# Context attention: VectorE multiplies the probabilities by the reciprocal, GpSimd keeps the power and the bias

## The chip, the cores and the metric

The kernel runs on one core of one Trainium2 chip. The metric is the device time of one execution in microseconds (us). The engines are TensorE (PE, with its weight loads shown apart as PEld), VectorE (DVE), ScalarE (ACT), GpSimd (POOL) and SyncE (SP), which here only issues DMAs.

## What is computed

Two layers of gated cross attention and feed forward work on x, 8 batches of 512 rows with 512 columns, all float32. The change lies in the attention of the second layer, which attends over a context of 77 rows:

```python
x = x + tanh(g_xattn[0]) * L0_xattn(layernorm(x), fside, fside, ctx, ...)
x = x + tanh(g_ffn[0]) * L0_ffn(layernorm(x), ...)
x = x + tanh(g_xattn[1]) * L1_xattn(layernorm(x), ctx, ctx, ...)
x = x + tanh(g_ffn[1]) * L1_ffn(layernorm(x), ...)

# L1_xattn: 16 heads of 32
q, k, v = split_heads(Q @ Wq.T + bq), split_heads(K @ Wk.T + bk), split_heads(V @ Wv.T + bv)
attn = softmax(einsum('bhqd,bhkd->bhqk', q, k) / sqrt(d_k), axis=-1)
return einsum('bhqk,bhkd->bhqd', attn, v) merged over heads @ Wo.T + bo
```

The keys and values of the context come from an earlier pass.

## The kernel before

The program is a row of passes, one after another with a barrier between them: the context, the first attention, the quantised feed forward, the context attention (`context_attention_pass`, the pass of the change, names beginning with `xat_` in the profile), the recurrence and the output.

**Tiles.** A batch has T = 4 row blocks of P = 128 rows and C = 4 column blocks of 128. The 16 heads go in 4 groups c of HG = 4 heads. One group of one batch is a quad, numbered i = b * 4 + c. Its scores, 128 partitions x 4 heads x 4 row blocks x 77, are 1232 values a partition.

**One quad.** TensorE makes the scores in PSUM (L2081). VectorE takes the maximum, negated (L2221), and adds it to the scores, into SM in SBUF (L2224). ScalarE takes the exponential into E (L2165). VectorE sums E (L2231) and takes the reciprocal RD (L2233). GpSimd multiplies E by RD, broadcast over the 77, into PR (L2030). TensorE transposes PR head by head into PSUM (L2090), ScalarE copies each into PT (L2150), and TensorE multiplies the values with it (L2070, the job "att"). SM, E, SU, RD and PR have two buffers each, taken in turn by c % 2.

**The other jobs.** "x" are transposes of the normalised rows XN of the next batch (L2057), "q" the query projection (L108, from XT and WQ), "out" the output projection (L108, from AT and WO). Float32 operands of a projection are held as a high and a low half: ScalarE copies the high half out of PSUM (L2136 for x, L2145 for att), VectorE subtracts it for the low half (L2215). Queries are taken out by ScalarE with their bias (L2142). For "out" VectorE adds the gated product to the rows in XR (L2210); it waits for s_bo, the bias being in XR. The products of all jobs share two PSUM banks, so that a job waits until what stood two jobs before it has been taken out.

**The order.** It is written out by hand. A turn is one batch, with groups c = 0 to 3. TURN says which jobs stand in which group, with the lag of their batch, and SLOT between which of the 4 heads' transposes:

```python
TURN = [[("att", 2, -1), ("q", 3, 0), ("x", 0, 1), ("x", 1, 1), ("x", 2, 1), ("x", 3, 1)],
        [("att", 3, -1), ("q", 0, 1), ("out", 0, -1), ("out", 1, -1)],
        [("out", 2, -1), ("out", 3, -1), ("att", 0, 0)],
        [("att", 1, 0), ("q", 1, 1), ("q", 2, 1)]]
```

In group c TensorE transposes the quad before and, behind slot 1, makes the scores of the next one, for which VectorE must have read the present ones (s_sub). VectorE's queue in a group is: maximum and subtract, the jobs of slots 0 and 1, sums and reciprocal, the jobs of slots 2 and 3, and at the end of group 1 the statistics of the rows two batches ahead (L573 to L582), at the end of group 3 their scaling (L587, four instructions of 128x512 from X to XN). Between these two GpSimd computes the power -0.5 of the variance (L561). ScalarE's exponential stands at the start of slot 1.

**Rows in and out.** XR holds the rows to which the output is added. SyncE stores a batch when its four out jobs are taken (L1972, in group 2 of the turn after), then loads the next rows into XR (L1988). GpSimd adds the gated output bias BO to all of XR (L2035) in group 3, behind its multiply. In the last turn it then computes the power for the next pass, whose first rows VectorE scales at the end of group 3.

**The loop.** `clock` runs the same `group(b, c)` on every engine: turn 0 written out, turns 1 to 5 as a loop on the engine, turns 6 and 7 written out, with jobs ahead and late around them.

Of the kernel before, what the change touches and what calls it, by code (L numbers as in the profile page):

```python
# [9 lines left out]
ALU = mybir.AluOpType  # L10
# [3 lines left out]
P = 128  # L14
B = 8
S = 512
D = 512
T = S // P
# [3 lines left out]
HG = P // DH  # L22
G = 77
# [8 lines left out]
def f32(ap):  # L32
    return ap.bitcast(F32)
# [79 lines left out]
def make_identity(pool, ident, sem):  # L113
    pool.memset(ident, 0.0).then_inc(sem, 1)
    pool.wait_ge(sem, 1)
    pool.affine_select(out=ident, in_=ident, compare_op=ALU.not_equal, fill=1.0, base=0,
                       pattern=[[-1, P]], channel_multiplier=1).then_inc(sem, 1)
# [1711 lines left out]
def context_attention_pass(nc, x2_s, g, bq, bo, k1_s, v1_s, x3_s, next_w, WQ, WO, X, XN, NEXT):  # L1829
# [23 lines left out]
    def jobs_of(turn, c):  # L1853

        here = MIDDLE if not isinstance(turn, int) else turn
        return [(kind, i, turn + lag) for slot in range(T) for kind, i, lag in TURN[c]
                if SLOT[kind, i] == slot and 0 <= here + lag < B]
# [22 lines left out]
    with Pass(nc, "xat") as ps:  # L1880
# [3 lines left out]
        BO = ps.sb("bo", [P, D])  # L1884
        TG = ps.sb("tg", [P, 2])
        XR = ps.sb("xr", [P, T, D])
# [7 lines left out]
        E = [ps.sb(f"e{i}", [P, HG * T, G]) for i in range(2)]  # L1894
        SU = [ps.sb(f"su{i}", [P, HG * T]) for i in range(2)]
        RD = [ps.sb(f"rd{i}", [P, HG * T]) for i in range(2)]
        PR = [ps.sb(f"pr{i}", [P, HG, T, G]) for i in range(2)]
# [7 lines left out]
        s_x, s_xr, s_v, s_store, s_dve = (ps.sem(n) for n in ("x", "xr", "v", "store", "dve"))  # L1905
# [3 lines left out]
        s_xhi, s_ahi, s_bo = (ps.sem(n) for n in ("xhi", "ahi", "bo_added"))  # L1909
        s_s, s_neg, s_sub, s_exp, s_sum, s_rd, s_nrm = (  # L1910
            ps.sem(n) for n in ("s", "neg", "sub", "exp", "sum", "rd", "nrm"))
        s_pt, s_pte = ps.sem("pt"), ps.sem("pte")
# [5 lines left out]
        def wait_some(eng, sem, value):  # L1918

            if not isinstance(value, int) or value > 0:  # L1920
                eng.wait_ge(sem, value)

        def bank(turn, job):
            return pj_ps[place(turn, job)[0] % 2][:]

        def clock(eng, group, ahead, late):

            ahead()
            for c in range(C):
                group(0, c)  # L1930
            with eng.Fori(0, B - 3) as i:
                for c in range(C):
                    group(i + 1, c)
            for b in (B - 2, B - 1):
                for c in range(C):
                    group(b, c)
            late()

        def quad(b, c):
            return b * C + c  # L1940
# [72 lines left out]
        @block.gpsimd  # L2013
        def _(pool):
            make_identity(pool, ident[:], s_ident)
            ln.pool_setup(pool)
            pool.sem_inc(ln.s_rstd, 1)

            def ahead():
                ln.pool_power(pool, 1)  # L2020
                pool.wait_ge(s_act0, 1)
                pool.tensor_scalar(BO[:], BO[:], TG[:, 1:2], None, ALU.mult).then_inc(s_pool, 1)
                pool.wait_ge(s_pool, 1)

            def group(b, c):
                last = isinstance(b, int) and b >= B - 2
                i = quad(b, c)
                pool.wait_ge(s_rd, i + 1)
                wait_some(pool, s_pt, i * HG - HG)
                pool.tensor_tensor(PR[c % 2][:].rearrange("p j t g -> p (j t) g"), E[c % 2][:],  # L2030
                                   RD[c % 2][:].unsqueeze(2).broadcast_to([P, HG * T, G]),
                                   ALU.mult).then_inc(s_nrm, 1)
                if c == 3:
                    pool.wait_ge(s_xr, b * 16 + 16)
                    pool.tensor_tensor(XR[:], XR[:], BO[:].unsqueeze(1).broadcast_to([P, T, D]),  # L2035
                                       ALU.add).then_inc(s_bo, 1)
                if c == 2 and not last:
                    ln.pool_power(pool, b + 2)
                if c == 3 and isinstance(b, int) and b == B - 1:
                    ln.pool_power(pool, B)  # L2040

            clock(pool, group, ahead, lambda: None)
# [155 lines left out]
        @block.vector  # L2198
        def _(dve):
            dve.sem_inc(s_dve, ln.DVE_N)  # L2200
            dve.sem_inc(ln.s_var, 1)

            def job(turn, task):

                kind, i, b = task
                src = bank(turn, task)
                if kind == "out":
                    dve.wait_ge(s_bo, b + 1)
                    dve.wait_ge(made["out"], b * C + i + 1)
                    dve.scalar_tensor_tensor(XR[:, i, :], src, TG[:, 1:2], XR[:, i, :],  # L2210
                                             ALU.mult, ALU.add).then_inc(taken["out"], 1)
                elif kind != "q":
                    halves, high = {"x": (XT, s_xhi), "att": (AT, s_ahi)}[kind]
                    dve.wait_ge(high, b * C + i + 1)
                    dve.tensor_tensor(halves[1][:, i, :], src, f32(halves[0][:, i, :]),  # L2215
                                      ALU.subtract).then_inc(taken[kind], 1)

            def minus_max(b, c):
                i = quad(b, c)
                dve.wait_ge(s_s, i + 1)  # L2220
                dve.tensor_reduce(MX[c % 2][:], s_v4, AX, ALU.max, negate=True).then_inc(s_neg, 1)  # L2221
                dve.wait_ge(s_neg, i + 1)
                wait_some(dve, s_exp, i - 1)
                dve.tensor_tensor(SM[c % 2][:], s_v4, MX[c % 2][:].unsqueeze(3).broadcast_to([P, HG, T, G]),  # L2224
                                  ALU.add).then_inc(s_sub, 1)

            def sums(b, c):
                i = quad(b, c)
                dve.wait_ge(s_exp, i + 1)
                wait_some(dve, s_nrm, i - 1)  # L2230
                dve.tensor_reduce(SU[c % 2][:], E[c % 2][:], AX, ALU.add).then_inc(s_sum, 1)  # L2231
                dve.wait_ge(s_sum, i + 1)
                dve.reciprocal(RD[c % 2][:], SU[c % 2][:]).then_inc(s_rd, 1)  # L2233

            def normalise(b, part, first=False):

                me = Steps(s_dve, b, ln.DVE_N)
                if part == 0:
                    dve.wait_ge(s_x, b * 16 + 16)
                    ln.moments(dve, me)  # L2240
                else:
                    me.done = 2 * T + 1
                    dve.wait_ge(made["x"], b * C)
                    ln.scale(dve, b, me)

            def next_low(n):

                dve.wait_ge(s_nexthi, n + 1)
                dve.tensor_tensor(NEXT[n][1][:], STAGE[:], f32(NEXT[n][0][:]), ALU.subtract).then_inc(s_nextlo, 1)

            def group(b, c):
                last = isinstance(b, int) and b >= B - 2
                jobs = jobs_of(b, c)
                minus_max(b, c)
                for j in range(HG):
                    if j == 2:
                        sums(b, c)
                    for task in jobs:
                        if SLOT[task[:2]] == j:
                            job(b, task)  # L2260
                    if not last and j == 3 and c in (1, 3):
                        normalise(b + 2, c // 2)
                at = (b - B + 2) * C + c if isinstance(b, int) else -1
                if 0 <= at < 6 and at % 2:
                    next_low(at // 2)
                if isinstance(b, int) and b == B - 1:
                    if c == 2:
                        dve.wait_ge(s_nextx, 16)
                        ln.moments(dve, Steps(s_next, 0, ln.DVE_N))
                    if c == 3:  # L2270
                        after = Steps(s_next, 0, ln.DVE_N)
                        after.done = 2 * T + 1
                        dve.wait_ge(made["x"], B * C)
                        ln.scale(dve, B, after)

            def ahead():
                for task in AHEAD:
                    job(-1, task)
                for part in range(2):
                    normalise(1, part)  # L2280
                dve.wait_ge(s_act0, 1)

            def late():
                for task in LATE:
                    job(B, task)

            clock(dve, group, ahead, late)
# [509 lines left out]
```

## Time and profile before

| | us |
|---|---|
| median of 3 runs (2578.31 to 2589.29) | 2588.45 |
| the profiled execution, its own time | 2587.03 |
| its span, first to last instruction | 2585.2 |
| busy: PE, DVE, ACT, POOL | 2362.0, 1443.2, 1060.5, 608.7 |
| mean granted clock of TensorE | 0.962 |

Columns of the groups below: start in us from the span's start, duration, engine and line, operation, the tiles it writes and reads, their sizes in partitions x elements, how many instructions a row merges, and in brackets how long the engine sat idle before it and what ended that. A granted clock of 1.00 is TensorE's level of 2.4 GHz, 0.50 that of 1.2 GHz.

### The profile page before, as it was taken

What the parts mean: (1) busy time and instruction counts of PE and PEld (TensorE: products, weight loads), DVE (VectorE), ACT (ScalarE), POOL (GpSimd) and SP (SyncE); (2) the same over time, 40 slices, a digit from 0 to 9 for tenths busy, and PEclk for the clock granted to TensorE, in tenths of its full rate; (3) what the DMA queues carried; (4) which work ended last, traced back from release to release, by engine and by line L of the source; (5) the groups of instructions that cost most, each with busy time, mean ns of one, the idle gap of its engine ahead of it and who ended that gap; (6) DMA issues with size and microseconds to landing.
All of it is one profiled execution on the core that took longest, in us unless ns stands there. A gap on an engine that the chain in (4) does not pass through costs nothing. (4 is left out here: it accounts for less than half of the span.)

```text
span 2585.2 us, 40732 instructions
## 1 busy us (share of the span) xinstructions
PE 2362.0 (91%) x16307; PEld 1554.4 (60%) x16348; DVE 1443.2 (56%) x1747; ACT 1060.5 (41%) x1228; POOL 608.7 (24%) x208
## 2 busy tenths in 40 slices
PE   8899999999999987899999878898878999999989
PEld 6655554555555543444444346676656888888867
DVE  7665646556565545777777567878544222222235
ACT  5444445444454442555554534444423221121223
POOL 0045546455464651000000013323210000000000
PEclk9899999999999988999999989999879999999999
DMA  9410101101010103111111131212322000000046
GB/s 298 178 40 12 49 10 48 43 11 47 10 48 11 56 15 123 34 50 49 49 53 38 38 112 44 83 56 87 106 85 82 33 32 26 22 32 32 17 156 218
DMA packets 102015, 163.73 MB, mean 63 GB/s; under 512 B 16997, under 2 KB 39525, under 8 KB 99103
## 3 DMA queue, kind: packets, MB, share of 16 engines
q1 hardware_dynamic: 95918, 150.82, 17.6%
q10 hardware_dynamic: 6000, 11.54, 1.2%
q8 instruction: 71, 1.16, 0.2%
q14 instruction: 26, 0.21, 0.0%
HBM read 112.63 MB, written 49.71 MB: 63 GB/s over the span
## 5 line engine op out<-in xcount | busy, mean ns | idle before, releaser
L1135 DVE TENSOR_REDUCE att_mx<-att_sn 128x2 f32<-128x1024 f32 x256 | 313.6, 1225 | 168.4 <-PE att_sn L947 166.0
L1047 ACT ACTIVATE att_num<-att_st 128x2048 f32<-128x2048 f32 x128 | 240.5, 1879 | 149.8 <-PE att_st L935 93.3
L860 POOL TENSOR_TENSOR att_es<-att_es,att_num 128x2048 f32<-128x2048 f32 x64 | 294.8, 4606 | 15.0 <-ACT att_num L1047 8.8
L856 POOL TENSOR_TENSOR att_es<-att_num 128x2048 f32<-128x2048 f32 x32 | 145.8, 4557 | 375.8 <-PE att_pj L917 366.4
L2508 ACT ACTIVATE rec_ga<-rec_g,rec_bg 128x512 f32<-128x512 f32 x84 | 57.1, 687 | 307.8 <-PE rec_g L2409 307.8
L2409 PE MATMUL rec_g<-weights_a_h,row_weights_h 128*128 128x512 f32 x384 | 152.9, 398 | 13.6 <-ACT rec_ga L2508 11.1
L2409 PE MATMUL rec_g<-weights_a_l,row_weights_h 128*128 128x512 f32 x384 | 151.7, 395 | 0.0
L2409 PE MATMUL rec_g<-weights_a_h,row_weights_l 128*128 128x512 f32 x384 | 151.5, 395 | 0.0
L947 PE MATMUL att_sn<-att_kh,att_qh 32*128 32x512 f32 x512 | 127.3, 493 | 22.7 <-DVE att_mx L1135 22.7
L1708 DVE TENSOR_TENSOR ffn_hs<-ffn_h,ffn_fb 128x1024 f32<-128x1024 f32 x64 | 78.1, 1220 | 117.5 <-PE ffn_h L1454 108.9
L561 POOL TENSOR_TENSOR ffn_ln_rstd<-ffn_ln_var,ffn_ln_power 128x4 f32<-128x4 f32 x8 | 22.0, 2755 | 484.0 <-DVE ffn_ln_var L582 484.0
L947 PEld LDWEIGHTS att_sn<-att_kh,att_qh 32*128 32x128 f32 x512 | 48.3, 185 | 143.0 <-DVE att_mx L1135 103.7
L2030 POOL TENSOR_TENSOR xat_pr<-xat_e,xat_rd 128x1232 f32<-128x1232 f32 x32 | 73.1, 2283 | 250.4 <-DVE xat_rd L2233 237.3
L1454 PE MATMUL ffn_h<-ffn_xqt,ffn_w 128*128 128x512 bf16 x486 | 117.0, 383 | 16.4 <-DVE ffn_hs L1708 12.9
L910 PE MATMUL att_pj<-att_num,att_v 128*32 128x512 f32 x1024 | 127.4, 618 | 0.9 <-DVE att_rd L1120 0.9
L1467 PE MATMUL ffn_c<-ffn_hs,ffn_dg 32*32 32x512 f32 x3072 | 114.7, 631 | 11.2 <-issue 4.6
L2573 DVE SCALAR_TENSOR_TENSOR rec_ga<-rec_ga,rec_c 128x512 f32<-128x512 f32 x32 | 22.1, 691 | 171.3 <-ACT rec_ga L2508 171.3
L561 POOL TENSOR_TENSOR rec_ln_rstd<-rec_ln_var,rec_ln_power 128x4 f32<-128x4 f32 x7 | 7.5, 1066 | 420.7 <-DVE rec_ln_var L582 420.7
L2150 ACT ACTIVATE xat_pt<-xat_pt 77x512 f32<-77x512 f32 x128 | 73.8, 588 | 77.4 <-PE xat_pt L2090 77.0
L1596 ACT ACTIVATE ffn_ss<-ffn_c,conv_bias 128x512 f32<-128x512 f32 x128 | 77.4, 692 | 66.6 <-PE ffn_c L1467 61.2
L1454 PEld LDWEIGHTS ffn_h<-ffn_xqt,ffn_w 128*128 128x128 bf16 x512 | 47.3, 99 | 84.8 <-issue 22.2
L2090 PEld LDWEIGHTS xat_pt<-xat_ident,xat_pr 128*77 128x77 f32 x512 | 67.1, 161 | 48.5 <-issue 23.4
(399 smaller groups left out, 5699.3 us busy)
## 6 DMA issues: line engine op xcount, KB each, us to landing
rows<-in_x SPq DMA_DIRECT2D x16, 1024.0 KB, 5.5
rows<-x SPq DMA_DIRECT2D x16, 1024.0 KB, 5.2
rows_b<-in_fside_BxSxS SPq DMA_DIRECT2D x8, 1024.0 KB, 7.9
heads<-att_o SPq DMA_DIRECT2D x32, 256.0 KB, 2.3
weights_b_l<-heads SPq DMA_DIRECT2D x8, 1024.0 KB, 5.2
x<-ffn_xr SPq DMA_DIRECT2D x32, 256.0 KB, 2.1
xat_xr<-x SPq DMA_DIRECT2D x8, 1024.0 KB, 5.1
out_x<-x SPq DMA_DIRECT2D x8, 1024.0 KB, 8.8
```

The source lines that it names most:

```text
L856: pool.tensor_tensor(ES[:], E[0][:], E[1][:], ALU.add).then_inc(s_sum, 1)
L860: pool.tensor_tensor(ES[:], ES[:], E[k][:], ALU.add).then_inc(s_sum, 1)
L910: last = pe.matmul(out[heads(j), :], V[:, k, c * P + DH * j:c * P + DH * j + DH], E[k][:, j, :], start=(k == 0), stop=(k == T - 1))
L947: last = pe.matmul(sn_ps[:, r, :], QT[0][c][own, m // 2 * P:m // 2 * P + P], KT[0][c][own, :], start=True, stop=True)
L1047: act.activation(E[k][:], st_ps[:], ACT.Exp, scale=SCALE).then_inc(s_exp, 1)
L1135: dve.tensor_reduce(MX[c % 2][:, m // 2, 2 * DH * (m % 2):2 * DH * (m % 2) + DH + 1:DH], sn_ps[:], AX, ALU.max, negate=True).then_inc(s_ma ...
L1454: last = pe.matmul(h_ps[:, m, :], W1[:, k, i * P:i * P + P], XQT[:, k, :], start=(k == 0), stop=(k == C - 1))
L1467: last = pe.matmul(c_ps[quarter(m), r, :], DG[quarter(r), 3 * (HG * group + m) + k, :], HS[group % 2][quarter(r), m, k:k + S], start=(k == ...
L1596: act.activation(SS[:, i, :], c_ps[:, r, :], ACT.Silu, bias=CB[:, i:i + 1]).then_inc(s_silu, 1)
L1708: dve.tensor_tensor(HS[group % 2][:, 2 * half:2 * half + 2, 1:S + 1], h_ps[:], FB[:].unsqueeze(1).broadcast_to([P, 2, S]), ALU.mult).then_ ...
L2150: act.activation(PT[d % 2][j][:], pt_ps[j % 2][0:G, :], ACT.Copy).then_inc(s_pte, 1)
L2409: last = pe.matmul(g_ps[m % 2][n][:], W[n][a][:, k, m * P:m * P + P], R[c][:, k, :], start=(part == 0 and k == 0 and i == 0), stop=((part ...
```

## The change

GpSimd's multiply goes to VectorE, right behind the reciprocal, with the same operands and buffers, the same semaphore (s_nrm) for those that wait for it, and the same wait on the transposes of two quads before (s_pt). VectorE now waits for its own reciprocal first. GpSimd keeps the power and the bias. The bias of batch b - 1 stands at group 0 of turn b in GpSimd's program, ahead of the power of that turn; that of the last batch stays in group 3 of the last turn, ahead of the last power.

```diff
--- before.py
+++ after.py
@@ -2022,18 +2022,17 @@
                 pool.tensor_scalar(BO[:], BO[:], TG[:, 1:2], None, ALU.mult).then_inc(s_pool, 1)
                 pool.wait_ge(s_pool, 1)
 
+            def bias_added(b):
+                pool.wait_ge(s_xr, b * 16 + 16)
+                pool.tensor_tensor(XR[:], XR[:], BO[:].unsqueeze(1).broadcast_to([P, T, D]),
+                                   ALU.add).then_inc(s_bo, 1)
+
             def group(b, c):
                 last = isinstance(b, int) and b >= B - 2
-                i = quad(b, c)
-                pool.wait_ge(s_rd, i + 1)
-                wait_some(pool, s_pt, i * HG - HG)
-                pool.tensor_tensor(PR[c % 2][:].rearrange("p j t g -> p (j t) g"), E[c % 2][:],
-                                   RD[c % 2][:].unsqueeze(2).broadcast_to([P, HG * T, G]),
-                                   ALU.mult).then_inc(s_nrm, 1)
-                if c == 3:
-                    pool.wait_ge(s_xr, b * 16 + 16)
-                    pool.tensor_tensor(XR[:], XR[:], BO[:].unsqueeze(1).broadcast_to([P, T, D]),
-                                       ALU.add).then_inc(s_bo, 1)
+                if c == 0 and not (isinstance(b, int) and b == 0):
+                    bias_added(b - 1)
+                if c == 3 and isinstance(b, int) and b == B - 1:
+                    bias_added(b)
                 if c == 2 and not last:
                     ln.pool_power(pool, b + 2)
                 if c == 3 and isinstance(b, int) and b == B - 1:
@@ -2231,6 +2230,11 @@
                 dve.tensor_reduce(SU[c % 2][:], E[c % 2][:], AX, ALU.add).then_inc(s_sum, 1)
                 dve.wait_ge(s_sum, i + 1)
                 dve.reciprocal(RD[c % 2][:], SU[c % 2][:]).then_inc(s_rd, 1)
+                dve.wait_ge(s_rd, i + 1)
+                wait_some(dve, s_pt, i * HG - HG)
+                dve.tensor_tensor(PR[c % 2][:].rearrange("p j t g -> p (j t) g"), E[c % 2][:],
+                                  RD[c % 2][:].unsqueeze(2).broadcast_to([P, HG * T, G]),
+                                  ALU.mult).then_inc(s_nrm, 1)
 
             def normalise(b, part, first=False):
 
```

## Rows read from the trace of the kernel before

**Rows 1.** Table of windows: busy per engine (instructions), clock, DMA share; stage, one turn.

```profile
1524.00:1928.00 404.00, 352.03 (x2678) 261.75 (x2676) 286.79 (x337) 170.08 (x259) 119.63 (x49) 0.93 0.23 77
...
1645.65:1691.30 45.65, 41.31 (x339) 31.04 (x337) 36.63 (x43) 20.42 (x32) 14.85 (x6) 1.00 0.24 76
```

**Rows 2.** Groups by line, and waits (total, times, longest), 1540 to 1930 us.

```profile
L2030 POOL TENSOR_TENSOR xat_pr<-xat_e,xat_rd 128x1232 f32<-128x1232 f32 x32 | 73.1, 2283 | 250.4 <-DVE xat_rd L2233 237.3 <-PE xat_pt L2090 13.1
...
PE xat_s L2081 <- DVE xat_sm L2224: 10.1, 11, 2.1
```

**Rows 3.** Time line of VectorE in a steady turn.

```profile
1652.11 1.40 DVE L2210 SCALAR_TENSOR_TENSOR xat_xr<-xat_pj,xat_tg,xat_xr 128x512 f32<-128x512 f32 x2
...
1661.86 8.08 DVE L587 TENSOR_SCALAR rows_b<-rows,xat_ln_mv,xat_ln_rstd 128x512 f32<-128x512 f32 x4
...
1671.42 1.44 DVE L2224 TENSOR_TENSOR xat_sm<-xat_s,xat_mx 128x1232 f32<-128x1232 f32 x1
...
1687.98 0.75 DVE L2210 SCALAR_TENSOR_TENSOR xat_xr<-xat_pj,xat_tg,xat_xr 128x512 f32<-128x512 f32 x1 [2.95 <-PE xat_pj L108]
```

**Rows 4.** Time line of VectorE: the same four scalings, GpSimd idle.

```profile
1532.68 1.92 DVE L587 TENSOR_SCALAR rows_b<-rows,xat_ln_mv,xat_ln_rstd 128x512 f32<-128x512 f32 x4 [1.22 <-POOL xat_ln_rstd L561]
```

**Rows 5.** Time line of GpSimd: first attention, the steady turn, the last turn.

```profile
920.91 11.07 POOL L860 TENSOR_TENSOR att_es<-att_es,att_num 128x2048 f32<-128x2048 f32 x2
...
1662.08 2.43 POOL L2030 TENSOR_TENSOR xat_pr<-xat_e,xat_rd 128x1232 f32<-128x1232 f32 x1 [3.49 <-DVE xat_rd L2233]
1664.48 4.73 POOL L2035 TENSOR_TENSOR xat_xr<-xat_xr,xat_bo 128x2048 f32<-128x2048 f32 x1
...
1901.64 4.50 POOL L2035 TENSOR_TENSOR xat_xr<-xat_xr,xat_bo 128x2048 f32<-128x2048 f32 x1
```

**Rows 6.** Time line of TensorE: the end of turn 0, then the steady turn.

```profile
1581.63 1.13 PE L2081 MATMUL xat_s<-xat_k,xat_qt 32*128 32x77 f32 x32 [0.49 <-DVE xat_sm L2224]
...
1657.75 0.66 PE L2090 MATMUL xat_pt<-xat_ident,xat_pr 128*77 128x128 f32 x4 [0.42 <-POOL xat_pr L2030]
...
1672.91 1.13 PE L2081 MATMUL xat_s<-xat_k,xat_qt 32*128 32x77 f32 x32 [0.62 <-DVE xat_sm L2224]
...
1676.57 1.25 PE L2057 MATMUL xat_pj<-xat_ident,rows_b 128*128 128x128 f32 x8 [0.65 <-DVE xat_xtl L2215]
```

**Rows 7.** Time line of VectorE: two operations with two SBUF operands elsewhere.

```profile
923.72 3.87 DVE L1219 TENSOR_TENSOR weights_b_l<-weights_b_l,weights_b_h 128x2048 fp32r<-128x2048 f32 x1
...
990.99 1.76 DVE L1682 TENSOR_TENSOR ffn_dg<-ffn_diagonal,conv_taps 128x1536 f32<-128x1536 f32 x1
```

**Rows 8.** Time line of SyncE, and DMA issues (KB each, us to landing), 1655 to 1672 us.

```profile
1658.78 0.37 SPq L1988 DMA_DIRECT2D xat_xr<-x  x1
...
xat_xr<-x SPq DMA_DIRECT2D x1, 1024.0 KB, 5.1
```

**Rows 9.** Time line of the stage's end: SyncE, TensorE, VectorE, TensorE.

```profile
1892.47 0.37 SPq L1988 DMA_DIRECT2D xat_xr<-x  x1
...
1901.74 3.81 PE L2090 MATMUL xat_pt<-xat_ident,xat_pr 128*77 128x128 f32 x16 [2.94 <-POOL xat_pr L2030]
...
1907.22 1.91 DVE L587 TENSOR_SCALAR rows_b<-rows,xat_ln_mv,xat_ln_rstd 128x512 f32<-128x512 f32 x4 [7.86 <-POOL xat_ln_rstd L561]
...
1910.48 0.77 PE L108 MATMUL xat_pj<-weights_b_h,xat_ath 128*128 128x512 f32 x1 [2.79 <-DVE xat_atl L2215]
```

**Rows 10.** TensorE in turn 7: time line, then windows (PE busy, clock, DMA).

```profile
1860.38 1.13 PE L2081 MATMUL xat_s<-xat_k,xat_qt 32*128 32x77 f32 x32 [2.15 <-DVE xat_sm L2224]
...
1866.33 1.99 PE L2090 MATMUL xat_pt<-xat_ident,xat_pr 128*77 128x128 f32 x8
...
1860.00:1861.00 1.00, 0.62 (x21) 1.00 0.00 0
1861.00:1862.00 1.00, 1.00 (x24) 0.87 0.06 16
1862.00:1863.00 1.00, 0.72 (x4) 0.50 0.00 0
...
1875.00:1876.00 1.00, 1.00 (x7) 0.81 0.00 0
```

## The prediction, made before the changed kernel was run

> **What bounds it now.** I read in this order: the table of windows, the groups by line, the waits, and then one steady turn on the time line, engine by engine. The stage of the change runs from 1524 to 1928 us, 404 of 2585 us. In it TensorE is busy 352 us and VectorE 287; inside one steady turn of 45.65 us TensorE is busy 41.3, VectorE 36.6, GpSimd only 14.9 [rows 1]. GpSimd's multiply, 32 of 2.28 us, is preceded by 250 us of idleness that VectorE ends, and TensorE's own waits are small items such as 10.1 us on VectorE's subtract [rows 2]. So GpSimd is no bound. What matters is the chain that goes round: TensorE's fourth output row block, VectorE's L2210, VectorE through groups 2 and 3, the scaling of the next rows (L587), the maximum and subtract of group 0, TensorE's scores, its transposes of the next rows.
>
> The steady turn shows it [rows 3]. VectorE's two L2210 end at 1653.5. It reaches L587 at 1661.86, and its four scalings take 8.08 us, to 1669.94; the same four alone took 1.92 us [rows 4]. The difference is GpSimd: its multiply ran from 1662.08 and the bias from 1664.48 to 1669.21, the multiply in 2.43 instead of 2.28 us on average, the bias in 4.73 where another took 4.50 alone [rows 5]. The two engines stand in each other's way, one instruction of each at a time. After L587 the subtract ends at 1672.86 and TensorE's scores, idle for 0.62 us, begin at 1672.91; later TensorE waits 0.65 us for VectorE's low halves before its third transpose block [rows 6]. These two gaps are where VectorE sets the pace of a turn.
>
> **The change, part by part.** GpSimd loses the multiply, VectorE gets it. No row shows it, but VectorE's subtract of the same 128x1232 takes 1.44 us [rows 3], and a product of two SBUF tensors of 128x1536 took 1.76 us [rows 7], which is 1.41 for 1232. Bounds 1.36 (the pitch of neighbours on the queue) to 1.5; I take 1.42 with the wait on the reciprocal. It also waits for s_pt, transposes of two groups earlier, long done: nothing. What is queued behind it on VectorE is the second half of a group: the low halves of att or of x, the output rows, and in group 3 the scaling.
>
> Group by group in the steady turn:
> - Group 1: behind the reciprocal VectorE idles 2.95 us for TensorE [rows 3]. The multiply lies in that: 0.
> - Group 2: on VectorE's chain from 1653.5 to L587: +1.42. The scores of group 0 ask for the subtract of group 3, which would end near 1660.1, over 1 us before they are issued: TensorE doesn't feel it.
> - Group 3: +1.42, directly ahead of L587. VectorE's multiply would run from 1663.3 to 1664.7.
> - The bias: on GpSimd nothing is ahead of it any more, so "a turn later" in the program is in fact when XR lands. XR's load is issued at 1658.78 and lands 5.1 us later, at 1663.9 [rows 8], in the middle of VectorE's multiply. Before, the bias began at 1664.48; so it comes hardly earlier, and lies ahead of all four scalings.
>
> Whether the multiply and the bias exclude each other decides 0.8 us. VectorE's subtract of two SBUF tensors of 128x2048 took 3.87 us where the rate of the 1536 wide product gives 2.35, and the two GpSimd additions beside it took 11.07 us, 2.0 more than twice 4.50 [rows 5, 7]. So I let them exclude each other. If they don't, the bias runs from 1663.9 to 1668.4 beside the multiply and the scaling ends at 1670.3, 0.8 us earlier than below. The Trainium skill (SBUF — State Buffer, "Who interferes with whom") states it as a rule: a VectorE instruction with two SBUF inputs, or in a two-port mode, and a GpSimd instruction that reads SBUF hold a shared port pair for the whole instruction, and the second blocks fully. The trace agrees with it in the rows just named, and it speaks against this change, since the multiply moves from one holder of the port to the other and cannot overlap the bias there.
>
> The scaling then: multiply to 1664.7, bias to 1669.2, four scalings of 1.92 to 1671.15, against 1669.94 before: +1.2. That is two multiplies in, +2.84, and from the end of the multiply to that of the scaling 6.45 us instead of 8.08, -1.63: GpSimd's multiply no longer stands in there, its bias still does.
> - Group 0: the scores are issued 1.2 us later. Between sums and low halves of x comes the next multiply, +1.42, and TensorE's third transpose block waits for that: +1.42 more.
>
> So a turn gets 1.2 + 1.4 = 2.6 us longer. TensorE gains the 0.42 us that it waits for GpSimd at 1657.75 [rows 6], but only to wait longer for the subtract. There are five such passages (turns 1 to 5 into the next turn): +13.0.
>
> Turn 0: XR was loaded long before, so the bias runs during group 2 and the scaling is alone: L587 in 1.9 instead of 8.0 us. But TensorE is behind there: groups 0 and 1 each put their multiply on the chain to the scores of group 3 (+2.8), VectorE's gain of 1.7 at the end of the scaling hides behind that, and TensorE gets back only the 0.49 us that it idled before the scores at 1581.63 [rows 6]: +2.3. Turns 6 and 7 have no next rows and VectorE idles between groups: 0. The end: TensorE waits 2.94 us for GpSimd's last multiply, until 1901.74 [rows 9]. VectorE's would be ready to start at 1900.8, but the last bias (XR's load, issued at 1892.47, lands near 1897.6) holds until 1902.1, so probabilities come at 1903.5, 1.8 later; in return the power is no longer behind the late bias, and the final scaling, which waited 7.86 us and held back the output's first product by 2.79, stops being late: net +0.5, between -2.3 (no exclusion) and +1.9.
>
> Sum without anything else: 2.3 + 13.0 + 0.5 = +15.8 us.
>
> **The clock.** TensorE's two gaps in group 0 grow from 0.62 to 2.2 us (0.62 + 0.42 + 1.2) and from 0.65 to 2.1, with 2.9 us of light work between. Where the trace has such a gap, the granted clock fell: 2.15 us of idleness before the scores at 1860.38, full clock until then, 0.87 in the microsecond from 1861, 0.50 after it, and 0.81 again only in that from 1875 [rows 10]. 0.50 is the level of 1.2 GHz, 1.00 that of 2.4. The steady turns with their gaps of 0.62 and 0.65 us stayed at 1.00 [rows 1]. So I expect a fall in most of the five turns. While it lasts, eight transposes take 1.99 us [rows 10] against 1.25 [rows 6]. A low stretch like that of 1861 to 1875 would catch the last 12 transposes of group 0 (+1.1), the att product and its transposes (+1.3) and ten products of q (some 2.0): 4.4 to 4.7 us; one that ends before the third transpose block costs 0. I take one in between that ends with the att product, 2.5 us: 5 x 2.5 = +12.5.
>
> **The likeliest case** is the chain and the clock together: +28.3 us on the profiled execution of 2587.03, whose span is 2585.2; 2615.3. The median of the runs shown is 1.4 above that execution, hence 2616.
>
> **Rivals.** (1) The chain without the clock: +15.8, 2604. For it: the gaps fall in a turn whose rest is dense, and a turn at 0.90 busy kept 1.00 [rows 1]. Against: the rows of the low stretches above. (2) On the other side: the scaling escapes the bias. If XR lands after VectorE has finished the scaling, L587 takes 1.92 us, ends near 1666.6, the subtract is ready before TensorE wants it, and the multiply in group 0 is done before the low halves of x are due; a turn loses its 0.62 and 0.42 us gaps, 5 x -1.04 + 2.3 + 0.5 = -2.4: 2586, no slowdown. It decides at a landing 2.3 us later than I reckon (over 7.4 us after its issue, against 5.1). Nothing delays that load, so it is unlikely. (3) Long low clock in every turn: 2.3 + 5 x (2.6 + 4.7) + 0.5 = +39.3: 2628. (4) Multiply and bias don't exclude each other: 5 x 1.8 + 2.3 - 2.3 = +9: 2598, and smaller gaps, so no fall.
> The move of program order alone changes no wait: the output rows ask for the bias a whole group after it is added, in both versions.
>
> **Numbers.** Likeliest (chain with clock) 0.50, its own range 2608 to 2624; (1) 0.18; (2) 0.12; (3) 0.13; (4) 0.07. A measurement of this kernel can tell about 0.5%, 13 us, from no change. (2), (4) and a little of (1) fall within it: 0.18. For a gain over 0.5% I found no mechanism and leave 0.06. Slower: 0.76. The range leaves out (2) and the upper half of (3): 2596 to 2630.
>
> **What the next profile would show.** VectorE gets 32 multiplies of 1.4 us; if they are longer in group 3, the bias came first. The four scalings in the steady turns: 6.5 us with a blocked first one (the forecast), 1.9 (rival 2). The turn's period: 48.2 us without and some 50.8 with falls of the clock, against 45.65. TensorE's idleness in group 0, before the scores and before the third transpose block: 2.2 and 2.1 us. The granted clock of the stage: below the 0.93 of before, with low stretches beginning in group 0. Wrong would be above all: a load of XR at another moment, or TensorE's gaps filled by work that I take to be behind them.

## The result and the profile after

| | before | after |
|---|---|---|
| median of 4 runs, us | 2587.15 | 2615.6 |
| lowest to highest, us | 2578.31 to 2589.29 | 2609.89 to 2617.83 |
| the profiled execution, us | 2587.03 | 2617.83 |
| its span, us | 2585.2 | 2616.0 |

The changed kernel is slower: the ratio is 1.0113, 95% interval 1.0084 to 1.0143. A second measurement of it on another occasion gave 1.0112, 1.0093 to 1.0131.

The stage again as a row of the table of windows, then the passage from the mark of turn 4 to that of turn 5 and the next one (the marks are explained below; columns as in rows 1: length, busy of PE, PEld, DVE, ACT, POOL with their instructions, granted clock, DMA share, GB/s). This is the changed kernel:

```profile
1524.00:1955.50 431.50, 363.03 (x2680) 271.09 (x2680) 322.48 (x371) 170.85 (x260) 50.30 (x17) 0.90 0.22 72
...
1763.31:1814.22 50.91, 44.04 (x338) 32.58 (x337) 40.46 (x46) 20.43 (x32) 6.17 (x2) 0.93 0.21 68
1814.22:1863.52 49.30, 42.65 (x345) 32.21 (x344) 39.71 (x38) 22.19 (x33) 5.27 (x1) 1.00 0.21 71
```

The second of these passages in the kernel before:

```profile
1787.63:1834.45 46.82, 42.66 (x345) 32.20 (x344) 35.94 (x34) 22.19 (x33) 14.84 (x6) 1.00 0.21 75
```

Against [rows 1] the stage is 27.5 us longer, GpSimd's busy time has fallen by 69 us and VectorE's has risen by 36, less than its 47 us of new multiplies. Where the clock falls behind the second of the two gaps shown below, a turn takes 50.9 us instead of 45.65; the passage at full clock takes 49.3 instead of 46.8, 2.5 more.

VectorE on the time line of one of these turns, changed kernel, answering [rows 3]:

```profile
1774.07 1.44 DVE L2230 TENSOR_REDUCE xat_su<-xat_e 128x16 f32<-128x1232 f32 x1 [0.70 <-ACT xat_e L2164]
1775.54 0.25 DVE L2232 RECIPROCAL xat_rd<-xat_su 128x16 f32<-128x16 f32 x1
1775.92 1.44 DVE L2235 TENSOR_TENSOR xat_pr<-xat_e,xat_rd 128x1232 f32<-128x1232 f32 x1
1777.28 6.14 DVE L587 TENSOR_SCALAR rows_b<-rows,xat_ln_mv,xat_ln_rstd 128x512 f32<-128x512 f32 x4
...
1784.90 1.44 DVE L2223 TENSOR_TENSOR xat_sm<-xat_s,xat_mx 128x1232 f32<-128x1232 f32 x1
...
1789.57 1.44 DVE L2235 TENSOR_TENSOR xat_pr<-xat_e,xat_rd 128x1232 f32<-128x1232 f32 x1
1790.93 1.28 DVE L2214 TENSOR_TENSOR xat_xtl<-xat_pj,xat_xth 128x512 fp32r<-128x512 f32 x2
```

The multiply takes 1.44 us and begins 0.38 us after the reciprocal's start, where the low halves used to follow by 0.2: with the wait it costs VectorE 1.5 us of its queue. The four scalings take 6.14 us, for GpSimd's bias still runs beside them. GpSimd, and the load before it, answering [rows 5] and [rows 8]:

```profile
1771.36 0.37 SPq L1988 DMA_DIRECT2D xat_xr<-x  x1
...
1776.62 5.15 POOL L2027 TENSOR_TENSOR xat_xr<-xat_xr,xat_bo 128x2048 f32<-128x2048 f32 x1 [13.62 <-DMA xat_xr<-x]
```

The bias waits for the load and for nothing else. It starts 5.26 us after the load's issue, in the middle of the multiply of 1775.92, and lasts 5.15 us instead of 4.50.

TensorE in the same passage, answering [rows 6], with the granted clock in windows of 1 us (PE busy, clock):

```profile
1786.39 1.13 PE L2080 MATMUL xat_s<-xat_k,xat_qt 32*128 32x77 f32 x32 [2.00 <-DVE xat_sm L2223]
...
1791.67 1.25 PE L2056 MATMUL xat_pj<-xat_ident,rows_b 128*128 128x128 f32 x8 [2.27 <-DVE xat_xtl L2214]
...
1791.00:1792.00 1.00, 0.33 (x3) 1.00 0.00 0
1792.00:1793.00 1.00, 1.00 (x10) 0.90 0.00 0
1793.00:1794.00 1.00, 0.78 (x4) 0.50 0.00 0
...
1799.00:1800.00 1.00, 1.00 (x5) 0.69 0.00 0
```

The gaps have grown to 2.00 and 2.27 us, and behind them TensorE's clock goes to its lower level (0.50, 1.2 GHz) for some 7 us. So it does in turns 3, 4 and 5. In turn 2 it falls one gap earlier, already behind the wait before the scores, and at the low clock TensorE then waits 0.52 us before the third transpose block instead of 2.27 (changed kernel):

```profile
1635.81 2.00 PE L2080 MATMUL xat_s<-xat_k,xat_qt 32*128 32x77 f32 x32 [2.00 <-DVE xat_sm L2223]
...
1641.08 1.82 PE L2056 MATMUL xat_pj<-xat_ident,rows_b 128*128 128x128 f32 x8 [0.52 <-DVE xat_xtl L2214]
...
1635.00:1636.00 1.00, 0.19 (x4) 0.89 0.93 301
1636.00:1637.00 1.00, 1.00 (x24) 0.50 1.03 403
...
1642.00:1643.00 1.00, 1.00 (x8) 0.69 0.00 0
```

In turn 6 the two gaps are 2.04 and 2.17 us, and the clock stays at 1.00.

**Where the time came from.** The start of VectorE's subtract is a mark that both traces have in every group (L2224 before, L2223 after). Their distance, read at the mark of group 2 in each turn, gives the loss turn by turn; the mark of the stage's end is GpSimd's first instruction of the next pass.

```
mark                          before     after   after - before   gained since the last
turn 0, group 0              1539.63   1541.59        +1.96
turn 1, group 2              1605.09   1612.73        +7.64        +5.68
turn 2, group 2              1650.75   1661.46       +10.71        +3.07
turn 3, group 2              1696.37   1712.38       +16.01        +5.30
turn 4, group 2              1742.00   1763.31       +21.31        +5.30
turn 5, group 2              1787.63   1814.22       +26.59        +5.28
turn 6, group 2              1834.45   1863.52       +29.07        +2.48
turn 7, group 2              1885.42   1913.56       +28.14        -0.93
first POOL row of next pass  1928.52   1956.13       +27.61        -0.53
end of span                   2585.2    2616.0       +30.8         +3.2
```

The five passages between turns cost 21.4 us, turn 0 5.7, the rest of the stage nothing or less. The 1.96 at the first mark was there before anything changed had run, and the 3.2 at the end come after the stage; both are taken up below.

### The profile page after: what moved, and what is told of

Its sections match the earlier page's. It is cut to its first block and busy times, and to the rows that moved or that the text cites. A ratio compares the mean times of both kernels' runs of the same rounds, so it can differ in the third digit from the quotient of the medians.

```text
span 2616.0 us, 40753 instructions
## 1 busy us (share of the span) xinstructions
PE 2381.1 (91%) x16348; PEld 1565.6 (60%) x16348; DVE 1477.0 (56%) x1779; ACT 1061.3 (41%) x1228; POOL 539.8 (21%) x176
## 5 line engine op out<-in xcount | busy, mean ns | idle before, releaser
L1454 PE MATMUL ffn_h<-ffn_xqt,ffn_w 128*128 128x512 bf16 x512 | 123.3, 384 | 12.9 <-DVE ffn_hs L1708 12.9
L2413 PEld LDWEIGHTS rec_g<-weights_a_h,row_weights_h 128*128 128x128 f32 x384 | 73.6, 192 | 32.4 <-ACT rec_ga L2512 12.6
```

The costliest lines, as they stand in the source:

```text
L1454: last = pe.matmul(h_ps[:, m, :], W1[:, k, i * P:i * P + P], XQT[:, k, :], start=(k == 0), stop=(k == C - 1))
L2413: last = pe.matmul(g_ps[m % 2][n][:], W[n][a][:, k, m * P:m * P + P], R[c][:, k, :], start=(part == 0 and k == 0 and i == 0), stop=((part ...
```

## The experiments

**One group at a time.** Each kernel is the kernel before with VectorE's multiply in one group only. Both engines then count up s_nrm, so each waits for the multiply before its own, long done by then.

```diff
+        def multiplied(eng, i, c):
+            eng.wait_ge(s_rd, i + 1)
+            wait_some(eng, s_nrm, i)
+            wait_some(eng, s_pt, i * HG - HG)
+            eng.tensor_tensor(PR[c % 2][:]..., E[c % 2][:], RD[c % 2][:]..., ALU.mult).then_inc(s_nrm, 1)
...
+                if c not in ON_VECTOR:
+                    multiplied(pool, i, c)
...
+                if c in ON_VECTOR:
+                    multiplied(dve, i, c)
```

Group 0 alone: 

> VectorE multiplies in group 0 alone, GpSimd in groups 1 to 3. Chain theory (the multiply counts only where VectorE's queue sets the turn): the low halves of x and the third transpose block come 1.4 us later, so a steady turn takes 47.1 us (45.65 + 1.42) with the clock up, TensorE's gap before the third transpose block 2.1 instead of 0.65, and up to 50 where the clock falls behind that gap. Load theory (VectorE's busy time is what counts, each group costs alike): a quarter of the 2.5 us that a turn with the clock up lost with all four groups moved, 46.3.

Group 1 alone: 

> VectorE multiplies in group 1 alone. Chain theory: it lies in VectorE's 2.95 us of waiting for TensorE, the steady turn stays at 45.65 and that waiting falls to 1.5. Turn 0, which has no output jobs, has no such slack in group 1 and may lose up to 1.4. Load theory: 46.3.

Group 2 alone: 

> VectorE multiplies in group 2 alone. Chain theory: it delays L587 by 1.42, GpSimd's multiply and bias still stand in the way of the scaling (8.1 us), so the steady turn takes 47.1 with the clock up; TensorE's gap before the scores of group 0 grows from 0.62 to 2.5, and the clock may fall behind it. Load theory: 46.3.

Group 3 alone: 

> VectorE multiplies in group 3 alone. Chain theory with exclusion: 1.42 us more ahead of L587, but GpSimd's multiply of 2.3 no longer interrupts the scaling, which falls from 8.1 to about 6.4 or 5.8; the turn stays within 0.3 us of 45.65, likeliest 45.4. Load theory: 46.3. The last transposes of the stage wait for VectorE instead of GpSimd, 2.9 us of TensorE's idleness at most 1.8 longer.

Measured by the same marks, in us over the kernel before (the turns from 1/group 2 to 6/group 2; the whole times are single ones and say little):

```
                     turn 0 to 1    five passages (each)            time of the one run (before: 2583.5)
only_g0                 +3.96       +2.70 +1.65 +2.73 +1.65 +2.64    2589.6
only_g1                 +2.91       +0.06 +0.10 +0.12 +0.09 +0.08    2589.43
only_g2                 +0.02       +1.56 +1.84 +1.98 +2.07 +2.17    2594.64
only_g3                 -1.09       -0.40 -0.35 -0.37 -0.36 -0.37    2579.11
all four (after)        +5.68       +3.07 +5.30 +5.30 +5.28 +2.48    2617.83
```

The first column is the less certain one: a second trace of the kernel before (twin, below) is 1.5 us behind it there with nothing changed, and within 0.1 us of it in the five passages. VectorE gets the same instruction in each of these kernels, and a turn pays 0.1 us for it in group 1, 1.65 in group 0 and more where the clock fell, about 2 in group 2, and gains 0.4 in group 3. The load theory, with a like share for each, is wrong. What makes group 1 free is VectorE's waiting for TensorE, 2.95 us before [rows 3] and less by the multiply in only_g1:

```profile
1644.14 1.44 DVE L1947 TENSOR_TENSOR xat_pr<-xat_e,xat_rd 128x1232 f32<-128x1232 f32 x1
...
1646.95 0.75 DVE L2216 SCALAR_TENSOR_TENSOR xat_xr<-xat_pj,xat_tg,xat_xr 128x512 f32<-128x512 f32 x1 [1.37 <-PE xat_pj L108]
```

In only_g0 the one gap of TensorE is there (time line of TensorE; only_g0):

```profile
1673.98 1.25 PE L2063 MATMUL xat_pj<-xat_ident,rows_b 128*128 128x128 f32 x8 [2.27 <-DVE xat_xtl L2221]
```

In only_g2 the scalings are blocked as before and only come later; in only_g3 they lose the multiply beside them, and the bias now blocks them alone. VectorE's L587 in only_g2, and L587 and the bias in only_g3:

```profile
1662.21 8.11 DVE L587 TENSOR_SCALAR rows_b<-rows,xat_ln_mv,xat_ln_rstd 128x512 f32<-128x512 f32 x4
```

```profile
1653.32 6.15 DVE L587 TENSOR_SCALAR rows_b<-rows,xat_ln_mv,xat_ln_rstd 128x512 f32<-128x512 f32 x4
...
1653.95 4.78 POOL L2041 TENSOR_TENSOR xat_xr<-xat_xr,xat_bo 128x2048 f32<-128x2048 f32 x1 [5.45 <-DMA xat_xr<-x]
```

**The bias behind the scaling.** If the multiplies hurt because the bias stands in front of the scaling, then holding the bias back must free them, with all four still on VectorE.

```diff
             def bias_added(b):
+                if not isinstance(b, int) or b < B - 2:
+                    pool.wait_ge(s_dve, (b + 3) * ln.DVE_N)
                 pool.wait_ge(s_xr, b * 16 + 16)
```

> The changed kernel with one wait more: GpSimd adds the bias of a turn only when VectorE has finished the scaling at the end of group 3. All four multiplies stay on VectorE. Port theory (the bias in front of the scaling is what puts the multiplies on the chain): L587 falls from 6.14 to 1.92 us, the scores of group 0 find their subtract ready, the multiply of group 0 ends before the low halves of x are due, TensorE's gaps of 2.0 and 2.3 us close, the clock stays up, and a steady turn takes 44.6 us, under the 45.65 of the kernel before; the whole about 2587 (5 x -1.0 and +5.7 for turn 0). Load theory (VectorE's 32 multiplies themselves are too much for its queue): the turn gets shorter by at most the 4.2 us of blocking in its five turns but stays above 45.65, the whole at 2600 or more.

Ratio 1.0009, 0.9992 to 1.0025: no slower than the kernel before. VectorE, GpSimd and TensorE on the time line of late_bias:

```profile
1655.78 1.44 DVE L2237 TENSOR_TENSOR xat_pr<-xat_e,xat_rd 128x1232 f32<-128x1232 f32 x1
1657.14 1.91 DVE L587 TENSOR_SCALAR rows_b<-rows,xat_ln_mv,xat_ln_rstd 128x512 f32<-128x512 f32 x4
...
1659.22 4.61 POOL L2029 TENSOR_TENSOR xat_xr<-xat_xr,xat_bo 128x2048 f32<-128x2048 f32 x1 [16.36 <-DVE rows_b L587]
...
1664.18 1.13 PE L2082 MATMUL xat_s<-xat_k,xat_qt 32*128 32x77 f32 x32
...
1667.31 1.25 PE L2058 MATMUL xat_pj<-xat_ident,rows_b 128*128 128x128 f32 x8 [0.54 <-DVE xat_xtl L2216]
```

The scaling takes 1.91 us, the scores wait for nothing, and the third transpose block waits 0.54 us although the multiply of group 0 stands in front of the low halves. From turn to turn the marks gain 1.68 us on the kernel before: 43.95 us, with 32 multiplies on VectorE. So VectorE has room for them; the order of the two engines at the scaling decides. Turn 0 still costs 4.9 us in this trace; the five passages gain 8.2 and turn 7 gains 2.2. The 44.6 us expected was 0.65 too long: it counted TensorE's gaps of 0.62 and 0.42 us, but a wait of 0.20 us for ScalarE's queries went too, the 0.65 us gap before the third transpose block shrank to 0.54, and TensorE's busy time in a turn fell from 41.28 to 40.95 us.

**The same hold without the change, and with half of it.** before_late adds the wait to the kernel before; g23_late also has groups 2 and 3 multiply on VectorE.

```diff
                 if c == 3:
+                    if not last:
+                        pool.wait_ge(s_dve, (b + 3) * ln.DVE_N)
                     pool.wait_ge(s_xr, b * 16 + 16)
```

> The kernel before, its four multiplies on GpSimd, with the bias waiting for the scaling. Port theory: GpSimd's multiply of group 3 still blocks one scaling, L587 takes 4.2 instead of 8.1 us, TensorE's 0.62 us before the scores of group 0 close, its 0.42 for GpSimd and 0.65 for the low halves stay: turn 45.0 us, about 2584. If the block by the bias was hidden anyway, turn 45.65 and no difference.

> VectorE multiplies in groups 2 and 3, GpSimd in 0 and 1, and the bias waits for the scaling. Port theory: scaling 1.92 us, no wait of TensorE for GpSimd in group 3 and none for the subtract in group 0; turn 44.6 us, turn 0 no longer than before; 5 x -1.0 in the steady turns, some 3 more in turn 0: about 2580 against 2587 of the kernel before. Load theory: half of the multiplies, half of the loss, 2600.

VectorE and GpSimd in before_late: one scaling is still blocked, by the multiply.

```profile
1659.13 3.85 DVE L587 TENSOR_SCALAR rows_b<-rows,xat_ln_mv,xat_ln_rstd 128x512 f32<-128x512 f32 x4
...
1659.35 2.44 POOL L2030 TENSOR_TENSOR xat_pr<-xat_e,xat_rd 128x1232 f32<-128x1232 f32 x1 [3.48 <-DVE xat_rd L2235]
```

By the marks a turn is 1.2 us shorter in before_late and 1.7 in g23_late; from the stage's first to its last mark they gain 5.7 and 8.8 us. But of that the whole shows little: ratios 0.9994 (0.9979 to 1.0009) and 1.0001 (0.9982 to 1.0019). 3 and 7 us less than the kernel before had been expected; the medians are 1.5 and 1.3 less (2581.6 and 2581.73 against 2583.05): no gain that can be measured. With the hold in both, all four multiplies on VectorE against none makes a turn 43.95 us instead of 44.43: it is with the bias in front of the scaling alone that they cost.

**TensorE kept busy.** Three of the five passages cost 5.3 us, the one without a fall 2.5. Is the difference the clock? In fill, the changed kernel, unused transposes of the identity fill most of the two gaps. They go to the transpose bank that has just been read.

```diff
+            def filled(n, j, turn):
+                if turn:
+                    pe.wait_ge(s_pte, turn[0] * H + HG * turn[1] + j - 1)
+                for _ in range(n):
+                    pe.transpose(pt_ps[j % 2][:, 0:P], ident[:], ident[:])
...
+                            if task[:2] == ("x", 2):
+                                filled(13, 3, probabilities)
...
+                    if j == 1 and c == 0 and not last:
+                        filled(12, 2, probabilities)
```

> The changed kernel with unused transposes of the identity on TensorE in group 0: 12 (about 1.7 us) ahead of the scores, 13 (about 1.8 us) ahead of the third transpose block of x, into the transpose bank that is free just then. They fill the two gaps and delay nothing there. Clock theory: without the idleness the granted clock stays at 1.00 in the steady turns, turns 2 to 4 take 48.1 us instead of 50.9, about 2607 against 2616. If those 2.8 us are not the clock's but another wait's, the turns stay at 50.9 or get longer. In turn 0, where the gaps are smaller, the transposes may delay TensorE by up to 2 us.

It ran twice; the second time, fill_again, beside the changed kernel (after_again) on the same chip:

> The changed kernel with the unused transposes in TensorE's gaps of group 0, beside after_again. If the falls of the clock in the stage cost the whole kernel its 8 to 10 us in every execution, this one is 0.3 to 0.4% faster than after_again. If they fall seldom in the executions that are timed without a profile, or if the rest of the kernel gives the time back, the two are equal within 0.15%. The turns are at 48.2 us each in either case.

> The changed kernel once more, beside fill_again and on the same chip. Chain and clock: turn 5 of its stage takes about 48.1 us and the turns in which the clock falls 50.9; which turns they are may differ from one execution to the next, since the traces so far show the fall in three of five. Whole: 1.1% over the kernel before.

TensorE on the time line of fill_again, then two of its turns in windows of 48.20 us:

```profile
1726.56 1.47 PE L2096 MATMUL xat_pt<-xat_ident 128*128 128x128 f32 x12
1728.74 1.13 PE L2080 MATMUL xat_s<-xat_k,xat_qt 32*128 32x77 f32 x32 [0.70 <-DVE xat_sm L2233]
...
1731.58 1.58 PE L2096 MATMUL xat_pt<-xat_ident 128*128 128x128 f32 x13
1734.01 1.25 PE L2056 MATMUL xat_pj<-xat_ident,rows_b 128*128 128x128 f32 x8 [0.84 <-DVE xat_xtl L2224]
...
1650.00:1698.20 48.20, 44.00 (x363) 33.74 (x362) 40.37 (x46) 20.44 (x33) 6.19 (x2) 1.00 0.23 72
1698.20:1746.40 48.20, 44.00 (x363) 33.79 (x362) 40.37 (x46) 20.44 (x33) 6.27 (x2) 1.00 0.22 72
```

The clock stays at 1.00 and all five passages cost 2.45 to 2.55 us over the kernel before, in both executions. Turns 2 to 4 are thus 2.8 us shorter each with TensorE doing more. after_again shows the falls in the same turns as the first trace (+3.10, +5.29, +5.31, +5.30, +2.48 us). Its ratio is 1.0112 (1.0093 to 1.0131), that of fill_again 1.0088 (1.0067 to 1.0109): 0.24% or 6 us between them (9 by the medians, 2604.29 and 2613.28), where the expected gain was 8 to 10. The intervals touch, so the whole times alone do not settle it; the stage in the traces is 8.3 us shorter (426.6 against 434.9 us). The first run of fill, at 1.011 (1.0077 to 1.0142) from 4 timings, did not show it.

**Equal kernels, and the held bias once more.** 

> The kernel before under another name. It says what equal kernels differ by: a ratio within 0.1% of 1. The part of its trace after the stage takes 656.6 us as in the kernel before if that is a matter of the program, and may take 659.8 if it is chance.

> The kernel before with the bias waiting for the scaling, once more. Its stage was 8.6 us shorter in the trace, the rest 3.3 us longer. If the rest takes 659.9 us because the stage ends earlier, its whole is 5 us (0.2%) under the kernel before; if the rest takes one of two values by chance, the mean over many runs shows 8 us (0.3%); if neither, no difference.

twin came to 1.0004 (0.9991 to 1.0017), before_late_again to 0.9995 (0.9986 to 1.0004), the last of its three expected outcomes: no difference.

twin also shows what a single trace is worth. Its marks against those of the kernel before: +1.49 us in turn 0, 0.0 to 0.1 in each of the five passages, -1.51 in turn 7, nothing in the sum. What differs is where TensorE's clock is low. In turn 0 the stretch lasts from 1554 to 1565 us in before and to 1568 in twin (windows of 2 us: two of before, two of twin):

```profile
1554.00:1556.00 2.00, 0.48 (x2) 0.63 0.00 0
1564.00:1566.00 2.00, 1.27 (x8) 0.81 0.01 4
...
1554.00:1556.00 2.00, 0.12 (x4) 0.58 0.00 0
1566.00:1568.00 2.00, 2.00 (x6) 0.51 0.00 0
```

and the low stretch of before from 1837 to 1845 us is missing in twin. fill and fill_again differ by 1.2 us in turn 0 (+5.63 and +6.82). So turns 0 and 7 are known to 1.5 us at best, the passages between turns to 0.1.

Ahead of the stage the traces of all kernels differ by up to 14 us, the stage beginning between 1509 and 1523 us, though nothing there was changed; before and after lie within 1.3 us of each other. What lies behind the stage takes one of few values:

```
from the first POOL row of the next pass to the end of the span, us
before 656.7, twin 656.2, only_g1 656.5, only_g2 656.7
only_g0 658.4
after 659.9, after_again 660.0, only_g3 659.7, late_bias 659.9, g23_late 659.8,
before_late 660.0, before_late_again 659.9, fill 659.7, fill_again 660.0
```

The four kernels with two traces repeat their value within 0.5 us, which speaks for a matter of the program and against chance; it is not one of the stage's length (400 or 435 us both go with 659.9). The moment at which the stage ends sorts them as well, though: from 1925 to 1936 us in those with 656 and in only_g0, 1911 to 1919 or 1944 to 1958 in those with 659.9. No run here separates the two. In the windows the granted clock differs: from 60 to 80 us behind the stage's end it is 0.91 in before and twin and 0.83 in those with 659.9, and from 550 to 600 us behind it 0.99 or 1.00 against 0.93. So of the 5.7 and 8.8 us that before_late and g23_late gain, 3.3 go back there. Of what is left, 2.4 us lie within the interval of before_late's ratio, which reaches down to 5.4 us less than before, and 5.5 us outside that of g23_late, which reaches down to 4.6; I cannot place them. What sets this clock stays open.

## Why the prediction was right

**The outcome.** 2616.0 was forecast, 2615.6 measured; the sum on the profiled execution, 2587.03 + 28.3, stands against 2617.83. Part of that closeness is luck. Between the first mark and the stage's end 25.7 us were measured where 28.3 were forecast, and the 5.2 us that lie outside (2.0 ahead, 3.2 behind) were no part of the forecast. Inside, turn 0 was put too low, the clock and the end too high.

**The multiply**, taken at 1.42 us with its wait: 1.44 and 1.5 with the wait. Group 1 at 0: only_g1 has 0.1 in the steady turns. Group 2 at +1.42: 1.6 to 2.2 in only_g2, where it stands before a scaling blocked for 8.11 us and the clock falls in each passage, for 4 to 5 us. Group 3 at 1.42 - 1.63 = -0.2: -0.4 in only_g3. Group 0 at +1.42: 1.65 with the clock up.

**The bias and the port.** XR's landing was put at 5.1 us behind its issue: 5.26. The scaling was forecast to take 6.45 us counted with the block, measured 6.14, since bias and scalings interleave. That multiply and bias exclude each other was argued from other stages; the last turn of the changed kernel shows it directly. The bias ran from 1925.75 to 1930.25, and VectorE's multiply, which takes 1.44 us elsewhere, took 2.59 and ended 1.3 us behind it:

```profile
1925.75 4.50 POOL L2027 TENSOR_TENSOR xat_xr<-xat_xr,xat_bo 128x2048 f32<-128x2048 f32 x1 [41.66 <-DMA xat_xr<-x]
...
1928.97 2.59 DVE L2235 TENSOR_TENSOR xat_pr<-xat_e,xat_rd 128x1232 f32<-128x1232 f32 x1
```

By the rule of the Trainium skill (SBUF — State Buffer, "Who interferes with whom") a VectorE instruction with two SBUF inputs and a GpSimd instruction that reads SBUF contend, and the one that issues second blocks; that row agrees with it.

**The chain of a turn**, +2.6: 2.48 in the passage without a fall and 2.45 to 2.55 in all of fill's. The gaps of 2.2 and 2.1 us: 2.00 and 2.27.

**The clock**, +2.5 in each of five passages: 2.8 in three, 0.6 in the first, 0 in the last, 9.0 together instead of 12.5. The price was nearly right where the fall came behind the second gap. It fell in four of the five, most turns as argued, but in the first behind the gap before the scores, where the low clock took the place of the wait before the third transpose block; and in the last passage the same two gaps left it at 1.00, so the gaps are not the whole condition. That it does not fall without them, fill shows.

**Turn 0**, +2.3: measured 5.7 (5.67 in after_again) against before, 4.2 against twin; by its ratio the worst of the terms on either count. Mis-sized was the +2.8 for two multiplies on the chain to the scores of group 3, and the clock of turn 0 was taken to stay as it was. In the changed kernel these scores start 23.20 us behind the first mark, against 19.42 in before and 19.43 in twin: 3.8 later. TensorE waits 2.60 us instead of 1.07 before the third transpose block of group 0, then 3.60 instead of 1.54 before the scores, and the clock falls behind each of the two waits; in the kernel before it falls once. TensorE on the time line of the changed kernel, then its clock:

```profile
1548.18 1.97 PE L2056 MATMUL xat_pj<-xat_ident,rows_b 128*128 128x128 f32 x8 [2.60 <-DVE xat_xtl L2214]
...
1564.79 2.01 PE L2080 MATMUL xat_s<-xat_k,xat_qt 32*128 32x77 f32 x32 [3.60 <-DVE xat_sm L2223]
...
1562.00:1564.00 2.00, 0.00 (x0) 1.00 0.00 0
1564.00:1566.00 2.00, 1.21 (x24) 0.53 0.00 0
...
1576.00:1578.00 2.00, 2.00 (x7) 0.56 0.00 0
1578.00:1580.00 2.00, 2.00 (x40) 1.00 0.00 0
```

From these scores to those of group 0 in turn 1 TensorE needs 14.3 us at the low clock, against 11.3 in before and 13.9 in twin; of its lead of 3.0 us the kernel before loses 1.1 again in the next two groups. What was forecast for turn 1, that its multiply of group 0 hides, came true: the low halves behind it waited for ScalarE and not for the multiply, and TensorE waited 0.54 us before that block, as in twin (0.66 in before).

```profile
1592.17 1.29 DVE L2214 TENSOR_TENSOR xat_xtl<-xat_pj,xat_xth 128x512 fp32r<-128x512 f32 x2 [0.35 <-ACT xat_xth L2135]
```

By groups I can't divide turn 0: only_g0 has +3.96 there, only_g1 +2.91 (no output jobs, so no slack in group 1), only_g3 -1.09, but each of these single traces carries the 1.5 us by which equal kernels differ, and that the three sum to 5.8 says nothing.

**The end**, +0.5, and turns 6 and 7 at 0: together -1.5 against before and 0.0 against twin. The last probabilities came at 1931.56, 1.8 us later than before when the 28.1 us of then are taken off, as forecast; the final scaling waited 0.99 us instead of 7.86, and the first product of the output 1.54 instead of 2.79.

**The rivals.** (1), the chain without the clock (2604, a ratio of 1.006), is what fill comes near to in the turns; its whole is 1.0088. (2), the scaling escaping the bias, needed a later landing by itself; late_bias makes it happen by a wait, and the outcome is the one it named, no slowdown: 2582.5 with the kernel before at 2583.05 on that occasion, where the rival had 2586 against 2588. (3) and (4) fell with the clock's short stretches and the 2.59 us row. What I did not see is the part behind the stage, 3.2 us.

## What to carry to other kernels

An engine with idle time has none for a new instruction at a given place until the place is looked at: the same 1.44 us multiply cost a turn 0.1, 1.65, 2 or -0.4 us, by the group it stood in, and whoever moves it should move it to where its engine waits for another. Where two engines exclude each other, look at the order of their instructions before their number: here one wait that holds GpSimd's bias behind VectorE's scaling took back the whole 1.1%, with all four multiplies left where the change had put them. And a gap of TensorE can cost more than its length if the clock falls behind it: 2.8 us more here in three passages, 0.6 in another, nothing in a fifth.

## What the runs showed of the hardware that I had not expected

- Two executions of the changed kernel had the clock's falls in the same turns, and each of the five passages agreed to 0.03 us. It is not so everywhere: before and twin, equal kernels, differ in the low stretches of turns 0 and 6. A fall behind gaps of some 2 us lasted 7 us; in only_g0, with one gap of 2.27 us, it came only in every other turn, lasted 4 us, and the whole passage cost 1.1 us more for it.
- 25 unused transposes in a turn, 3 us of work, made that turn 2.8 us shorter.
- A part of the program that was not touched, with 656 to 660 us of its own, takes 3.3 us more in some kernels than in others, and the same again in a second trace of the same kernel. What sets it is not shown.
- On VectorE the multiply, which waits for the reciprocal ahead of it (0.25 us long), starts 0.38 us after that one's start, where the low halves, which don't wait for it, started after 0.2.
